# Message rows that carry the one-hot of their node, gathered over a zero fill, in place of one-hots made on VectorE

## The reference, cut to what matters

```python
h = concatenate([x[src], x[dst]], axis=-1)
msgs = silu(h @ W1.T + b1) @ W2.T + b2
agg = segment_sum(msgs, src, 50000) / (count + 1e-08)
gi, gh = agg @ w_ih.T + b_ih, x @ w_hh.T + b_hh     # r, z, n: three parts of 256
r, z = sigmoid(i_r + h_r), sigmoid(i_z + h_z)
n = tanh(i_n + r * h_n)
x_new = (1 - z) * n + z * x
y = layernorm(x + gamma * normalised(x_new) + beta)
```

## Time and profile before

| what | us |
|---|---|
| median of 3 runs (lowest, highest) | 2310.09 (2299.78, 2317.37) |
| the profiled execution | 2299.15 |
| its span in the trace | 2297.3 |
| edge stage in the trace, about | 25 to 920 |
| node stage: first to last weight load of the segment sums | 942.7 to 2264.1 |

### The profile page before, as it was taken

How to read it: one execution, slowest core, us unless ns; L and a number is a source line. 1 busy time by engine, 2 the same in 40 slices (tenths; PEclk the granted TensorE clock), 3 DMA queues, 4 the chain that set the end, 5 groups by cost and what they waited for, 6 DMA issues and landing times.

```text
span 2297.3 us, 49749 instructions
## 1 busy us (share of the span) xinstructions
PE 2171.4 (95%) x10816; PEld 1663.7 (72%) x10816; DVE 2039.8 (89%) x6522; ACT 1559.6 (68%) x3158; POOL 1538.7 (67%) x1577
## 2 busy tenths in 40 slices
PE   5999999999999998699999999999999999999995
PEld 2888888888888887477666676767766766666673
DVE  5888888888888887499999999999999999999998
ACT  2454545454545454478888888888888878888887
POOL 4544444444444441488888888888888888888885
PEclk9999999999999999899999999999999999999997
DMA  4676677676666674567677676766677776767763
GB/s 137 231 247 245 245 245 247 245 245 245 246 245 245 244 246 196 207 211 240 232 235 231 236 241 233 237 229 233 227 234 231 234 225 227 240 230 230 231 227 133
DMA packets 200159, 527.52 MB, mean 230 GB/s; under 512 B 52392, under 2 KB 61248, under 8 KB 200128
## 3 DMA queue, kind: packets, MB, share of 16 engines
q1 hardware_dynamic: 124024, 320.32, 40.0%
q0 software_dynamic: 75264, 206.47, 27.4%
q10 hardware_dynamic: 840, 0.40, 0.1%
HBM read 475.16 MB, written 206.78 MB: 297 GB/s over the span
## 4 chain that ended last, share of the span: by engine, by line
PE 39%; DVE 22%; DMA 16%; issue 14%; POOL 6%; DVEq 1%; POOLq 0%; ACT 0%; SPq 0%; ACTq 0%
PE banks L1004 36%; DMA mg<-messages,rows_now 14%; PE banks L1020 4%; DVE tg L946 3%; DVE st L982 3%; POOL mg L378 3%; DVE zd L934 3%; DVE uu L957 3%; DVE oh L908 2%; DVE diff L929 2%; POOL rs L467 1%; POOL xb L451 1%; DVE npre L923 1%; DVE ag L988 1%; DVE nmr L977 1%
## 5 line engine op out<-in xcount | busy, mean ns | idle before, releaser
L1004 PE MATMUL banks<-whh,xts 128*128 128x512 f32 (+1 forms) x1568 | 561.3, 485 | 0.0
L378 POOL DMA_INDIRECT mg<-messages,rows_now x392 | 450.1, 1148 | 94.3 <-issue 78.4
L378 POOL DMA_INDIRECT xsrc<-in_x,src_now x196 | 186.8, 953 | 393.2 <-PE banks L1020 387.7
L1004 PE MATMUL banks<-mg,oh 128*128 128x512 f32 (+1 forms) x1568 | 322.3, 348 | 65.3 <-DVE npre L923 37.4
L1004 PEld LDWEIGHTS banks<-whh,xts 128*128 128x128 f32 x1568 | 269.2, 189 | 151.8 <-issue 141.3
L1004 PEld LDWEIGHTS banks<-mg,oh 128*128 128x128 f32 x1568 | 253.1, 189 | 171.0 <-issue 115.6
L523 ACT ACTIVATE msg<-banks 128x512 fp32r<-128x512 f32 (+1 forms) x392 | 192.7, 492 | 247.3 <-PE banks L1004 218.9
L593 ACT ACTIVATE banks<-banks,rcount 128x768 f32<-128x768 f32 x392 | 326.7, 871 | 28.8 <-PE banks L1004 19.2
L706 DVE TENSOR_TENSOR msg<-banks,msg 128x512 fp32r<-128x512 f32 (+1 forms) x392 | 199.9, 552 | 96.1 <-ACT msg L523 96.1
L1004 PE MATMUL banks<-wsh,silh 128*128 128x512 f32 (+1 forms) x784 | 265.7, 339 | 2.7 <-DVE msg L706 2.7
L599 ACT ACTIVATE nt<-npre 128x512 f32<-128x512 f32 x196 | 124.0, 632 | 210.0 <-DVE npre L923 210.0
(11 more groups left out here) (144 smaller groups left out, 5406.6 us busy)
## 6 DMA issues: line engine op xcount, KB each, us to landing
messages<-msg SPq DMA_DIRECT2D x196, 772.0 KB, 3.3
xts<-in_xt SPq DMA_DIRECT2D x196, 256.0 KB, 6.4
xs<-in_x SPq DMA_DIRECT2D x196, 256.0 KB, 3.5
out_y<-yy SPq DMA_DIRECT2D x196, 256.0 KB, 3.7
near<-tile_blocks SPq DMA_DIRECT2D x49, 128.0 KB, 4.5
mg<-messages,rows_now POOLq DMA_INDIRECT x392, 7.4
xsrc<-in_x,src_now POOLq DMA_INDIRECT x196, 4.0
xdst<-in_x,dst_now POOLq DMA_INDIRECT x196, 3.2
```

The source lines that it names most:

```text
L378: nc.gpsimd.indirect_dma_start(out=dst_tile, out_offset=None, in_=rows, in_offset=bass.IndirectOffsetOnAxis(ap=table, axis=0), bounds_chec ...
L1004: return nc.tensor.matmul(out_, lhsT, rhs, start=start, stop=stop, skip_group_check=skip)
```

## The change

A message row carries its one-hot itself. It is now 768 high values, 768 low values and 128 columns from HOT on: 1664 floats, 6656 bytes. `edge_local` writes these 128 columns on VectorE, in place of the single LOC column. The gather brings them with the row, and `segment_sum` takes its weights from `mg[:, u, h, HOT:ROW]`; `oh` and `one_hot` are gone. Since a gather leaves the rows of empty slots untouched, SyncE first lays zeros over the 128 columns of rows 0 to 125 of both blocks, from a tile `zeros` in SBUF, with one transfer per pair (from the second use of a buffer on), and then the counts into rows 126 and 127. The gather of a pair waits for both. `load_counts` becomes `load_one_hots`, one pair further ahead and at the head of SyncE's list. TensorE waits for the gathers itself, and `copy_rows` waits for the gathers that last read its tile. Two memsets of the padding columns go.

```diff
-LOC = G3
-HALF = G3 + 4
-ROW = 2 * HALF
+HALF = G3
+HOT = 2 * G3
+ROW = HOT + P
...
-            def load_counts(q, u):
-                need(sp, S["n_sg1"], q - QU + 1)
-                sp.dma_start(oh[SLOTS:P, u, :, :].bitcast(f32),
+            def load_one_hots(q, u):
+
+                if not isinstance(q, int) or q >= QU:
+                    for h in range(2):
+                        sp.wait_ge(S[f"n_sg{h}"], q - QU + 1)
+                    sp.dma_start(mg[0:SLOTS, u, :, HOT:ROW].bitcast(f32), zeros[0:SLOTS, :, :]).then_inc(got_c[u], 16)
+                sp.dma_start(mg[SLOTS:P, u, :, HOT:ROW].bitcast(f32),
                              counts[:, bass.ds(q * (2 * P), 2 * P)].rearrange("r (h l) -> r h l", h=2)).then_inc(got_c[u], 16)
...
-            node_turns(sp, ((store_y, -8), (load_counts, 3), (load_x, 3), (load_rows, 2)), first=-4, last=8)
+            sp.wait_ge(mg_zero, 2 * QU)
+            sp.wait_ge(zeros_ready, 1)
+            node_turns(sp, ((load_one_hots, 4), (store_y, -8), (load_x, 3), (load_rows, 2)), first=-4, last=8)
...
                 def copy_rows(q, u):
                     if u % 2 == 0 and not summed:
-                        need(pool, S["n_oh"], q - QU + 2)
+
+                        if not isinstance(q, int) or q >= QU:
+                            for v in range(4):
+                                pool.wait_ge(got_m[2 * u + v], 16 * nth(q, u))
...
                 def gather_rows(q, u):
                     if u % 2 == 0 and not summed:
                         pool.wait_ge(idx_now, 2 * E_TURNS + duo(q, u))
+                    pool.wait_ge(got_c[u], 32 * nth(q, u) + 16)
...
-                nc.vector.tensor_copy(msg[:, u % EU, LOC:LOC + 1], locf[:, bass.ds(slot(g, u), 1)]).then_inc(e_loc, 1)
+                nc.vector.tensor_scalar(msg[:, u % EU, HOT:ROW], iota1[:, :], locf[:, bass.ds(slot(g, u), 1)], None,
+                                        ALU.is_equal).then_inc(e_loc, 1)
...
-            def one_hot(q, u):
-                for h in range(2):
-                    need(dve, S[f"n_sg{h}"], q - QU + 1)
-                    dve.wait_ge(got_m[2 * u + h], 16 * (nth(q, u) + 1))
-                    last = nc.vector.tensor_scalar(oh[0:SLOTS, u, h, :], iota1[0:SLOTS, :],
-                                                   mg[0:SLOTS, u, h, LOC:LOC + 1].bitcast(f32),
-                                                   slot_used[0:SLOTS, bass.ds(q * 2 + h, 1)], ALU.is_equal, ALU.mult)
-                last.then_inc(S["n_oh"], 1)
-
...
             def segment_sum(q, u):
-                pe.wait_ge(S["n_oh"], q + 1)
-                pe.wait_ge(got_c[u], 16 * (nth(q, u) + 1))
                 need(pe, S["n_npre"], q - 1)
                 for h in range(2):
-                    segment_products(h, pn[u % 2], oh[:, u, h, :], mg[:, u, h, :]).then_inc(S[f"n_sg{h}"], 1)
+                    pe.wait_ge(got_m[2 * u + h], 16 * (nth(q, u) + 1))
+                    segment_products(h, pn[u % 2], mg[:, u, h, HOT:ROW], mg[:, u, h, :]).then_inc(S[f"n_sg{h}"], 1)
```

More of the change, by code:

```diff
@@ L105, in gnn_layer @@
         halves = sb("halves", [P, 4])
+        zeros = sb("zeros", [P, 2, P])
         top, levf, levi = sb("top", [P, 1]), sb("levf", [1, 1]), sb("levi", [1, 1], i32)
@@ L116, in gnn_layer @@
         slot_bits, slot_parts = sb("slot_bits", [P, 3, BLOCKS], i32, until=early), sb("slot_parts", [P, 4, BLOCKS], until=early)
+        oh_level = sb("oh_level", [P, P], f32r, until=early)
         eh, el = (sb(n, [P, 2, 2 * KC, SPAN], f32r, until=early) for n in ("eh", "el"))
@@ L120, in gnn_layer @@
         xsrc, xdst = (sb(n, [P, XE, D], until=early) for n in ("xsrc", "xdst"))
+        near = sb("near", [P, 2, SPAN], fp16, until=early)
+        same = sb("same", [P, P], fp16, until=early)
         silh, sill = (sb(n, [P, 2, KC, SPAN], f32r, until=early) for n in ("silh", "sill"))
@@ L127, in gnn_layer @@
         up_to_tile, later = sb("up_to_tile", [P, 2], until=early), sb("later", [P, 2], until=early)
-        near = sb("near", [P, 2, SPAN], fp16, until=early)
-        same = sb("same", [P, P], fp16, until=early)
         picked = sb("picked", [P, BLOCKS], fp16, until=early)
@@ L149, in gnn_layer @@
         mg = sb("mg", [P, QU, 2, ROW], f32r)
-        oh = sb("oh", [P, QU, 2, P], f32r)
         rz = sb("rz", [P, 2, 2, 2 * D])
@@ L183, in gnn_layer @@
         t_step, tab_ready, rc_step, rc_ready = sem("t_step"), sem("tab_ready"), sem("rc_step"), sem("rc_ready")
-        node_const, mg_zero = sem("node_const"), sem("mg_zero")
+        node_const, mg_zero, zeros_ready = sem("node_const"), sem("mg_zero"), sem("zeros_ready")
         lv_top, lv_row, lv_ready = sem("lv_top"), sem("lv_row"), sem("lv_ready")
@@ L193, in gnn_layer @@
         got_x, got_xt, got_m, n_stored = sems("got_x", QU), sems("got_xt", QU), sems("got_m", 2 * QU), sems("n_stored", QU)
-        names = ("n_oh n_sg0 n_sg1 n_sc0 n_sc1 n_g0 n_g1 n_mm n_rz0 n_rz1 n_rhn n_npre n_tanh n_diff n_xb n_zd n_xn"
+        names = ("n_sg0 n_sg1 n_sc0 n_sc1 n_g0 n_g1 n_mm n_rz0 n_rz1 n_rhn n_npre n_tanh n_diff n_xb n_zd n_xn"
                  " n_xh n_xl n_s1 n_a1 n_v1 n_r1 n_tg n_u n_nm2 n_sq2 n_v2 n_r2 n_nmr n_y").split()
@@ L402, in _ @@
             nc.gpsimd.memset(halves[:, :], -0.5).then_inc(node_const, 1)
+            nc.gpsimd.memset(zeros[:, :, :], 0.0).then_inc(zeros_ready, 1)
             with pool.Fori(0, E_TURNS // 2) as g:
@@ L486, in _ @@
                 pool.wait_ge(v_done, 1)
-                pool.wait_ge(tab_ready, 2)
                 node_stage(True)
@@ L792, in bias_step @@
                 if n == QUAD + 3:
-                    dve.wait_ge(node_const, 3)
+                    dve.wait_ge(node_const, 1)
                     dve.wait_ge(rb_step, 6)
@@ L841, in _ @@
                 dve.wait_ge(v_zero, 1)
-                nc.vector.tensor_copy(put[:, LOC:LOC + 1], cst[:, C_PART:C_PART + 1]).then_inc(v_zero, 1)
+                nc.vector.tensor_copy(put[:, HOT:ROW], ident).then_inc(v_zero, 1)
                 dve.wait_ge(v_cn, 1)
@@ L883, in _ @@
                         dve.wait_ge(v_got, n * 16 + 16)
-                        nc.vector.tensor_scalar(oh[:, 0, 0, :], iota1[:, :], mg[:, 0, 0, LOC:LOC + 1].bitcast(f32),
-                                                slot_used[:, bass.ds(b, 1)], ALU.is_equal, ALU.mult)\
-                            .then_inc(v_one, 1)
+                        nc.vector.tensor_scalar(oh_level[:, :], mg[:, 0, 0, HOT:ROW].bitcast(f32),
+                                                slot_used[:, bass.ds(b, 1)], None, ALU.mult).then_inc(v_one, 1)
                         dve.wait_ge(v_sum, n + 2)
@@ L997, in _ @@
             node_turns(dve, ((gated_h, -1), (aggregate1, -2), (n_input, -1), (shift, -7), (var_eps2, -5), (var_eps1, -2), (residual, -4), (minus_mean, -4),
-                             (subtract_n, -1), (z_diff, -1), (x_new, -1), (one_hot, 2), (scale_gamma, -3), (stats1, -1)),
+                             (subtract_n, -1), (z_diff, -1), (x_new, -1), (scale_gamma, -3), (stats1, -1)),
                        first=-2, last=7)
@@ L1139, in _ @@
                         pe.wait_ge(v_one, lv * BLOCKS + b + 1)
-                        segment_products(0, pn[1], oh[:, 0, 0, :], mg[:, 0, 0, :]).then_inc(v_sum, 1)
+                        segment_products(0, pn[1], oh_level[:, :], mg[:, 0, 0, :]).then_inc(v_sum, 1)
             def segment_sum(q, u):
-                pe.wait_ge(S["n_oh"], q + 1)
-                pe.wait_ge(got_c[u], 16 * (nth(q, u) + 1))
                 need(pe, S["n_npre"], q - 1)
                 for h in range(2):
-                    segment_products(h, pn[u % 2], oh[:, u, h, :], mg[:, u, h, :]).then_inc(S[f"n_sg{h}"], 1)
+                    pe.wait_ge(got_m[2 * u + h], 16 * (nth(q, u) + 1))
+                    segment_products(h, pn[u % 2], mg[:, u, h, HOT:ROW], mg[:, u, h, :]).then_inc(S[f"n_sg{h}"], 1)
             def node_products(q, u, h):
```

5 lines of the change are left out of this document (removed).

## The result

| | median us (lowest to highest) | ratio to before [95% interval] |
|---|---|---|
| before | 2309.06 (2299.78 to 2317.37) | |
| after | 2401.69 (2396.77 to 2404.17) | 1.041 [1.038, 1.044] |
| predicted | 2252 (2220 to 2325) | 0.975 |

The change costs 92.6 us, 4.1%. The prediction had the wrong sign. The third rival, slower by the chain of the zero fill, is what happened, and its 2363 us was still 39 us too low.

A forecast was written before the change was run, and what follows sets the result against it. VectorE was taken to bound the node stage, TensorE following closely; 195 steps times 0.29 us gave 57 us off 2299, so 2242 us profiled, plus 10 for the median: 2252 us, range 2220 to 2325.

The forecast's parts named there:

- The third rival: Node stage: fill lands as late as xts or later, at L = 8.2 step 7.1 us, time 2363 us; chance 0.13.
- I take L = 5.8, nearer to the store of y: Node stage: fill and counts land 5.8 us after the end of GpSimd's xb, so mostly no one waits.
- two steps need at least L + 6.0: GpSimd, node stage: landing time L after xb's end, plus some 6.0 us from gather start to next xb's end.
- The loop: Node stage: xb lets SyncE issue fill and counts; GpSimd's gather waits for them, and the next xb stands behind it.
- the limit of L: Node stage: at 6.48 us per step nothing is lost up to L = 6.96 us.
- The second rival: Node stage: xts lands 1.4 us later, ScalarE is late, step back to about 6.7 us, some 2295 us; chance 0.07.
- TensorE's floor: Node stage: shortest step TensorE allows once VectorE's one-hots go, 6.36 to 6.53 us, taken as 6.42.
- The forecast step of 6.48: Node stage: TensorE's 6.42 us plus 0.06 for irregular steps, 0.29 us less per pair than before.
- The edge stage: `edge_local` writes 128 columns for one, 0.1 to 0.2 us more each, costed at nothing under TensorE that never stops.
- The gathers' 3.5 us of slack: Node stage: a gather may land up to 3.5 us later than before without anyone waiting.
- The fill's weight on the engines: Node stage: 252 packets per pair cost 0.3 to 1.0 us on each DMA engine; share 0.8 (0.77 to 0.9).
- no one waits: Node stage: the forecast case, the fill mostly holds nothing up and TensorE sets the pace; chance 0.66.

The follow-up runs named there:

- the first: The changed kernel without the zero fill: SyncE issues only the counts, and the gather waits for them alone; 2254.88 us, ratio 0.978.
- the third run: The changed kernel with fill and counts issued one pair further ahead, behind the load of xts in SyncE's list; 2267.64 us, ratio 0.984.
- the link moved by a step: The changed kernel with load_rows at lag 1 in place of 2, so the fill is sent behind an xb one step earlier; 2256.34 us, ratio 0.978.
- the second run: The changed kernel with the fill going to a contiguous scratch tile, waited for by no gather, the counts still behind it; 2361.21 us, ratio 1.024.

## Why the prediction was wrong, and where it was right

**The step that failed** is "I take L = 5.8, nearer to the store of y", and with it a term that "two steps need at least L + 6.0" put at nothing. The loop itself was right, and so was its part after the gather: 5.41 us in the pair of steps shown, 6.21 in the next (1516.48 to 1522.69), 5.93 in the mean of 163. But from xb's end to the start of a gather that waits, the step of 7.32 us leaves 2 x 7.32 - 5.4 to 6.2 = 8.4 to 9.2 us. In the 86 pairs whose gather waited over 0.5 us this was 9.0 in the mean: L = 8.2, where I took 5.8 and the third rival 8.2, and 0.85 from the landing to the gather's start. Four things made up the difference.

- *The start of a gather that waited.* It begins 0.81 to 1.02 us after the semaphore is complete, in all 86 pairs. Where nothing holds it, it begins 0.17 us after xb, and I took no more. With it the limit of L at 6.48 us per step isn't 6.96 but about 6.1.
- *The issue.* I let the fill take the place of the store of y, with 0.36 us of issue. It took 0.87 us, and the counts came 1.07 to 1.10 us behind the fill. With the fill mostly 0.57 to 1.2 us after xb's end, the counts go out at +1.6 to +2.3, not at the +1.35 of the prediction.
- *The landing.* I bounded it by 3.7 and 6.4 us of other transfers and went to the lower end. By the trace's semaphore events fill and counts had landed 6.0 us after the fill's issue in the median (3.7 to 10.1 us).
- *A typical L put into a formula that wants the late ones.* Landings alternate. A gather that starts on time puts its packets on the engines just when the next fill goes out, and that fill is late. The gather that waited for it starts late, and the fill after that has the engines to itself. The landing events bear this out: 7.1 us after issue in the median for the 82 fills whose step's first gather had started by 0.3 us after them, 4.8 for the 81 others. Successive landings of the fill have a correlation of -0.64. An early landing gives nothing back, since GpSimd has other work until then. The mean L was 6.9 us, and 9.4 or more in one pair of ten. With the mean alone the step would be (6.9 + 0.85 + 5.93) / 2 = 6.84 us; the rest up to 7.32 I put down to only the late ones counting. So of the 0.84 us by which the step is over the forecast 6.48, about 0.36 come from the size of the terms and 0.48 from the alternation; no run separated them.

GpSimd's gathers go with later landings of SyncE's fill: it lands in 6.8 us in the median with both gathers of a step started from 1.5 us before it to 2.5 us after it (107 fills), and in 5.1 with none (29). By the Trainium skill (DMA: Bandwidth & Descriptors, Issuing engines are not separate DMA queues) transfers started by different engines run on the same DMA engines and interleave there; these two medians agree. The fit of the same page of the Trainium skill (Anatomy of one DMA) is given there for transfers that GpSimd issues, and the fill is SyncE's. The estimate by it, 2.3 us for this transfer, is 3.7 us under the measured median. The prediction had set it aside.

**The second rival** (xts late) was no rival but an addition. xh waited for xts in 103 steps of the kernel after. Its price, taken where the loop is out of the way, is 24 us with the fill's transfer (the runs with the fill ahead) and 17 us without it (2238.91 - 2221.47). I had sized it by one typical landing, as above, and put it at nothing in the sum. It doesn't make the loss: with xts at the head of the list that wait is 2.3 us and the kernel is at its slowest.

**Where the time lies,** from the kernel with ScalarE's zeros up to the kernel after:

| from, to | us | what |
|---|---|---|
| 2239 to 2268 | 29 | the fill as a transfer, out of the loop, in place of ScalarE's copy: its traffic and issues |
| 2268 to 2292 | 24 | xts behind the fill |
| 2292 to 2402 | 110 | the fill in the loop |

With the link moved by a step the last line is 145 us (2401.69 - 2256.34). In that version xh waits for xts only 37.4 us in 33 times, so most of the 24 us of the line above may be in it too. How the 35 us between the two numbers divide was not separated.

**What was right.** VectorE's one-hots were the bound, and TensorE the next. The forecast for TensorE's floor was 6.36 to 6.53 us, taken as 6.42. Measured: (2186.7 - 1.2 - 940.7) / 195 = 6.38 us, with TensorE busy 200 us of 200. The forecast step of 6.48 appeared with ScalarE's zeros, (2200.8 - 1.2 - 937.8) / 195 = 6.47. The kernel with the link moved makes every transfer of the change without the late loop, and its 2256 us lie near the forecast 2252. A part of that is luck: its step is 6.57 us and not 6.48, and the 10 us that I added for the median over the profiled execution aren't there (2256.34 and 2256.68). The edge stage cost nothing: 128 columns took 0.28 us each where one took 0.15, as estimated, under TensorE. The gathers' 3.5 us of slack held, since no wait of size for a gather appears on TensorE. The fill's weight on the engines was forecast at 0.3 to 1.0 us per pair. Between the first and the third run the share of SyncE's queue rose from 41.1% to 45.1%:

```profile
q1 hardware_dynamic: 175488, 357.15, 45.1%
```

That makes 0.451 x 16 x 2265.3 - 0.411 x 16 x 2253.7 = 1526 us for 175,488 - 124,416 = 51,072 packets, 30 ns each, or 0.5 us per pair on each engine, if the other packets took as long in both. The DMA share was 0.76 to 0.77 there, where the forecast had 0.77 to 0.9.

**What I should have done with it.** The prediction knew the loop, its limit (6.96) and its bounds (5.05 to 7.75). The limit lay inside the bounds, and xts, issued from the same queue, landed in 6.4. A chance of 0.66 for "no one waits" was not to be had from these rows.

## What to carry to other kernels

A transfer that is put into a closed loop (an engine's result lets the queue go on, the queue issues it, the same engine waits for its landing) is priced by its late landings and by the start of what waits for it, not by its median: an early one gives nothing back. Before adding one, ask what the queue's instruction ahead of it waits for; here a third step for the same loop, by one pair of lead or by one number in a lag, was worth 134 to 145 us. Where the data is a constant, an engine with idle time may lay it for less than the queue can: 0.40 us of ScalarE per pair, in time that it had free, stood against 29 to 163 us of the whole time.

## What the runs showed of the hardware that I had not expected

- The time to issue a transfer from SyncE goes neither by its bytes nor by its pieces alone: 0.33 us for 256 KB in 128 rows (xs), 0.60 us for 128 pieces of 512 bytes (half the fill), 0.87 us for 252 such pieces, and 0.81 us for 126 pieces of 1024 bytes (the second run). The fills between two tiles in SBUF cost SyncE more than the larger load from DRAM. Why isn't shown.
- A gather of GpSimd's that waited for a semaphore began 0.81 to 1.02 us after it was complete; one whose semaphores were complete began 0.17 us after the instruction before it.
- A transfer of 126 KB landed after 3.7 to 10.1 us, later with the gathers beside it: a spread of more than twice, in a kernel whose DMA share was 0.73.
- With waits of several us in the loop TensorE's granted clock fell to 0.98, and to 0.96 in the slowest kernel (2535 us), where TensorE was busy 168 us of 200. In the fastest (199 of 200 busy) it was 1.00. The mean of 0.98 is made of the two levels: from 1000 to 2150 us the kernel after has 11 spells of 3.4 us at 1.2 GHz, and 2.4 GHz for the rest. Each spell begins within 1.5 us of the end of an idle time of TensorE of 1.9 to 2.2 us. Sixteen other such idle times brought none. The kernels before and with the fill ahead have neither in this window. That the idle time brings the lower clock is likely from this order, but no run held one fixed and changed the other.
